# Four row tiles of attention probabilities: a fifth chunk of keys through the squares instead of TensorE's turns

## The reference

```python
def attention(x, ctx, wq, wk, wv, wo):      # per batch
    q, k_new, v_new = x @ wq.T, x @ wk.T, x @ wv.T
    k = concatenate([ctx, k_new])           # 512 + 512 keys
    v = concatenate([ctx, v_new])
    p = softmax(q @ k.T / sqrt(512))        # the mask is all false and not used
    return (p @ v) @ wo.T
x = x + tanh(g_xattn) * attention(layernorm(x), ...)
h = relu(layernorm(x) @ sign(up).T * up_scale)
x = x + tanh(g_ffn) * (h @ sign(down).T * down_scale) * output_scale
```

## Time and profile before

| | |
|---|---|
| median of three runs | 579.07 us |
| the profiled execution | 578.94 us |
| its span, from the first to the last instruction | 577.1 us |
| mean granted TensorE clock | 0.999 of full speed (2.4 GHz) |
| busy: TensorE, its weight loads | 571.5 us, 474.7 us |
| busy: VectorE, ScalarE, GpSimd | 397.4 us, 281.1 us, 125.7 us |
| DMA | 59.97 MB, 93248 packets, 71840 of them under 512 bytes |

### The profile page before, as it was taken

The page is one execution under the profiler, slowest core; times in us unless marked ns, Lnnn a source line. Parts: engine busy times, 40 slices in busy tenths (PEclk is TensorE's granted clock), DMA queues, the critical chain, the costliest instruction groups (busy, mean ns, idle before and its releaser), DMA issues.

```text
span 577.1 us, 6906 instructions
## 1 busy us (share of the span) xinstructions
PE 571.5 (99%) x2610; PEld 474.7 (82%) x2610; DVE 397.4 (69%) x556; ACT 281.1 (49%) x402; POOL 125.7 (22%) x111
## 2 busy tenths in 40 slices
PE   9999999999999999999999999999999999999997
PEld 7888888888888888888888888888888888888885
DVE  5889646688685588683588686777569645766654
ACT  3783513464321564321565454756468355555531
POOL 5006222102033002033002033332322022422002
PEclk9999999999999999999999999999999999999999
DMA  8711752124414145425113833273910311330011
GB/s 290 244 69 33 187 182 74 35 75 109 111 65 82 40 180 146 109 76 73 57 53 104 247 124 109 92 164 110 212 44 36 147 37 37 108 112 36 6 67 74
DMA packets 93248, 59.97 MB, mean 104 GB/s; under 512 B 71840, under 2 KB 75936, under 8 KB 92832
## 3 DMA queue, kind: packets, MB, share of 16 engines
q1 hardware_dynamic: 93216, 59.54, 35.4%
HBM read 44.84 MB, written 14.69 MB: 103 GB/s over the span
## 4 chain that ended last, share of the span: by engine, by line
PE 97%; DVE 1%; DMA 0%; ACT 0%; issue 0%
PE proj L680 28%; PE score L796 20%; PE turn L781 13%; PE score L714 9%; PE score L680 8%; PE turn L680 8%; PE proj L781 5%; PE proj L714 4%; PE score L922 2%; PE turn L672 1%; PE score L672 1%; DVE rows L1787 1%; DMA rows<-in_x 0%; DVE scaled L1784 0%; DVE stats L1615 0%; PE score L929 0%
## 5 line engine op out<-in xcount | busy, mean ns | idle before, releaser
L796 PE MATMUL score<-down_signs,hid_split 128*128 128x512 f32 x512 | 133.3, 389 | 0.0
L796 PEld LDWEIGHTS score<-down_signs,hid_split 128*128 128x128 f32 x512 | 96.0, 188 | 20.3 <-DVE hid_split L1668 0.5
L680 PE MATMUL proj<-four_x,weights 128*128 128x512 f32 x336 | 76.8, 389 | 0.0
L680 PEld LDWEIGHTS proj<-four_x,weights 128*128 128x128 f32 x336 | 63.0, 188 | 13.0
L604 POOL TENSOR_TENSOR four_x<-raw_ctx,four_x 128x2048 fp32r<-128x2048 f32 x7 | 32.6, 4656 | 132.0 <-ACT four_x L1010 132.0
L1668 DVE TENSOR_TENSOR hid_split<-hid,hid_split 128x512 fp32r<-128x512 f32 x64 | 44.4, 697 | 15.4 <-ACT hid_split L1226 15.1
L781 PE MATMUL turn<-ops_b,up_ops 128*128 128x512 f32 x192 | 51.3, 389 | 0.0
L1226 ACT ACTIVATE hid_split<-hid 128x512 fp32r<-128x512 f32 x64 | 40.0, 629 | 20.8 <-PE score L796 17.9
L1217 ACT ACTIVATE hid<-hid,hid_gain 128x512 f32<-128x512 f32 x48 | 34.7, 724 | 22.7 <-DVE hid L1697 11.1
L680 PE MATMUL score<-weights,four_x 128*128 128x512 f32 x192 | 45.3, 389 | 0.0
L680 PE MATMUL proj<-weights,four_x 128*128 128x512 f32 x192 | 45.3, 391 | 0.0
(11 more groups left out here) (140 smaller groups left out, 928.1 us busy)
## 6 DMA issues: line engine op xcount, KB each, us to landing
raw_w<-in_ffn_w SPq DMA_DIRECT2D x21, 512.0 KB, 3.3
raw_ctx<-in_ctx_turned SPq DMA_DIRECT2D x4, 1024.0 KB, 5.3
raw_ctx<-in_ctx SPq DMA_DIRECT2D x4, 1024.0 KB, 6.5
probs_rows<-probs_squares SPq DMA_DIRECT2D x64, 64.0 KB, 1.9
squares_placed<-probs_rows SPq DMA_DIRECT2D x8, 512.0 KB, 4.2
raw_x<-block_rows SPq DMA_DIRECT2D x4, 1024.0 KB, 7.3
result<-rows SPq DMA_DIRECT2D x16, 256.0 KB, 2.1
rows<-in_x SPq DMA_DIRECT2D x3, 1024.0 KB, 9.3
```

What stands on the lines that cost most here:

```text
L680: last = pe.matmul(bank, lhs(l), rhs(r), start=start and i == 0, stop=stop and i == 2)
L796: last = pe.matmul(wide(r), hid_split[:, n % HR, s, r * P:(r + 1) * P], down_signs[:, chunk_of(q), :], start=(q == 0 and s == HI), stop=(q ...
```

## The change

FAR gives each row tile the number of key chunks that go by the squares: five for all four, so the fifth is the first chunk of new keys. TensorE turns three chunks of a tile. `probs_squares` moves to another place of the memory, where the query parts lie, grows from 512 to 640 columns and for this its first write waits for another product of the scores. The loads of `squares_placed` have five chunks, and the second half is split by ScalarE and VectorE in two steps of one row tile each, so the counts of `placed_hi` and `placed_lo` become three per batch. The sync queue stores three tiles, loads the first half, stores the fourth tile and loads the second half. ScalarE's first split no longer waits for the stores. On TensorE the new product makes terms 1 to 3 of all four outputs first, then waits for the squares, and then makes the moved term 0 of all four, ahead of the context product.

```diff
--- before.py
+++ after.py
@@ -160,17 +160,23 @@
         late_squares = normed
 
 
+        FAR = dict.fromkeys(range(RT), RT + 1)
+        FAR_ALL = RT + 1
         PAIRS = ((2, 3), (0, 1))
-        probs_squares = at("probs_squares", 160, [P, RT, ROWS])
+        probs_squares = at("probs_squares", 112, [P, RT, FAR_ALL * P])
         squares_placed = at("squares_placed", 176, [P, KC, ROWS])
-        probs_rows = nc.dram_tensor("probs_rows", (BATCH, ROWS, ROWS), F32).ap()
+        probs_rows = nc.dram_tensor("probs_rows", (BATCH, FAR_ALL * P, ROWS), F32).ap()
         probs_rows_v = probs_rows.rearrange("b (c p) q -> b p c q", p=P)
         probs_squares_v = probs_rows.rearrange("b (j n) (t i a) -> b t i n j a", n=SQ, i=P // SQ, a=SQ)
 
         def placed_part(h):
 
             first = PAIRS[h][0] * P
-            return slice(None), slice(0, RT), slice(first, first + 2 * P)
+            return slice(None), slice(0, FAR[PAIRS[h][0]]), slice(first, first + 2 * P)
+
+        def split_part(k):
+
+            return placed_part(0) if k == 0 else (slice(None), slice(0, FAR_ALL), slice((k - 1) * P, k * P))
 
         def scaled(c, r):
 
@@ -230,6 +236,9 @@
                 return proj[:, n - 2, :] if n >= 2 else turn[:, n, :]
 
             return turn[:, n % 4, :] if n % 4 < 2 else score[1][:, n % 4 - 2, :]
+
+        def turned_cols(n):
+            return 4 * P if n < RT else KEYS - FAR[TILE_ORDER[n % RT]] * P
 
         def proj_bank(n):
             if n < DC:
@@ -450,18 +459,27 @@
 
             def place_squares(b):
 
-                for h, pair in enumerate(PAIRS):
-                    for t in pair:
-                        sp.wait_ge(probs_squared, tile_done(b, t))
-                        for i in range(P // SQ):
-                            sp.dma_start(probs_squares_v[b, t, i], probs_squares[i * SQ:(i + 1) * SQ, t].rearrange(
-                                "n (j a) -> n j a", a=SQ)).then_inc(squares_stored[h], 16)
+                def store_tile(t):
+                    sp.wait_ge(probs_squared, tile_done(b, t))
+                    far = FAR[t] * P // SQ
+                    for i in range(P // SQ):
+                        sp.dma_start(probs_squares_v[b, t, i][:, 0:far],
+                                     probs_squares[i * SQ:(i + 1) * SQ, t, 0:far * SQ].rearrange("n (j a) -> n j a", a=SQ)
+                                     ).then_inc(squares_stored[t not in PAIRS[0]], 16)
+
+                def place(h):
+                    sp.wait_ge(squares_stored[h], 2 * STORED * (b + 1))
+                    first, last = PAIRS[h]
+                    sp.dma_start(squares_placed[placed_part(h)],
+                                 probs_rows_v[b][:, 0:FAR[first], first * P:(last + 1) * P]).then_inc(placed[h], 16)
+
+                for t in TILE_ORDER[:3]:
+                    store_tile(t)
 
                 sp.wait_ge(scored, product_scored(b, A22, 1))
-                for h, pair in enumerate(PAIRS):
-                    sp.wait_ge(squares_stored[h], 2 * STORED * (b + 1))
-                    cols = slice(pair[0] * P, (pair[1] + 1) * P)
-                    sp.dma_start(squares_placed[placed_part(h)], probs_rows_v[b][:, :, cols]).then_inc(placed[h], 16)
+                place(0)
+                store_tile(TILE_ORDER[3])
+                place(1)
 
             def block_rows_back(b):
                 sp.wait_ge(squares_out[b], STORED)
@@ -673,7 +691,7 @@
                 last.then_inc(turned, 1)
 
             def cols(src):
-                return [src[:, k * P:(k + 1) * P] for k in range(4)]
+                return [src[:, k * P:(k + 1) * P] for k in range(src.shape[1] // P)]
 
             def product(bank, lhs, rhs, start, stop):
                 for i, (l, r) in enumerate(PASSES):
@@ -754,7 +772,7 @@
             def turn_probs(b, i):
                 t = TILE_ORDER[i]
                 pe.wait_ge(exp_done, tile_done(b, t))
-                turn_job(turn0(b) + i, cols(probs[:, t, ROWS:KEYS]))
+                turn_job(turn0(b) + i, cols(probs[:, t, FAR[t] * P:KEYS]))
 
             def v_jobs(b):
 
@@ -861,17 +879,20 @@
                 n = proj0(b)
                 pe.wait_ge(turn_lo, turn0(b) + RT)
 
+
                 for e in range(DC):
                     if e == 1:
                         pe.wait_ge(proj_lo, values_out(b, 3))
-                    for i, (lhs, rhs) in enumerate(new_terms(e)):
+                    for i, (lhs, rhs) in enumerate(new_terms(e)[1:]):
                         if e == 0:
 
-                            pe.wait_ge(proj_lo, values_out(b, max(i, 2)))
+                            pe.wait_ge(proj_lo, values_out(b, max(i + 1, 2)))
                         last = product(proj_bank(n + DC + e), lhs, rhs, i == 0, False)
+                pe.wait_ge(placed_lo, 3 * b + 3)
+                for e in range(DC):
+                    last = product(proj_bank(n + DC + e), *new_terms(e)[0], False, False)
                 if last_batch:
                     last.then_inc(new_read, 1)
-                pe.wait_ge(placed_lo, 2 * b + 2)
                 pe.wait_ge(ctx_ready, values_split(b) + 1)
                 for e in range(DC):
                     for i, (lhs, rhs) in enumerate(old_terms(e)):
@@ -1011,7 +1032,7 @@
 
             def turn_out(n, dst):
                 act.wait_ge(turned, n + 1)
-                act.activation(dst, four(turn_bank(n)), ACT.Copy).then_inc(turn_hi, 1)
+                act.activation(dst, four(turn_bank(n)[:, 0:turned_cols(n)]), ACT.Copy).then_inc(turn_hi, 1)
 
             def proj_out(n, dst):
                 act.wait_ge(proj_done, n + 1)
@@ -1093,15 +1114,13 @@
 
             def probs_out(b, i):
                 t = TILE_ORDER[i]
-                turn_out(turn0(b) + i, probsT[:, HI, RT:KC, t * P:(t + 1) * P])
+                turn_out(turn0(b) + i, probsT[:, HI, FAR[t]:KC, t * P:(t + 1) * P])
 
             def placed_out(b, h):
                 act.wait_ge(placed[h], 16 * (b + 1))
-                part = placed_part(h)
-                if h == 0:
-
-                    act.wait_ge(squares_stored[1], 2 * STORED * (b + 1))
-                act.activation(probsT[:, HI][part], squares_placed[part], ACT.Copy).then_inc(placed_hi, 1)
+                for k in ((0,), (1, 2))[h]:
+                    part = split_part(k)
+                    act.activation(probsT[:, HI][part], squares_placed[part], ACT.Copy).then_inc(placed_hi, 1)
 
             def take_signs(n):
                 kind, i = SIGNS[n]
@@ -1301,7 +1320,7 @@
 
             def turn_out(n, dst):
                 dve.wait_ge(turn_hi, n + 1)
-                dve.tensor_tensor(dst(LO), four(turn_bank(n)), dst(HI).bitcast(F32), ALU.subtract
+                dve.tensor_tensor(dst(LO), four(turn_bank(n)[:, 0:turned_cols(n)]), dst(HI).bitcast(F32), ALU.subtract
                                   ).then_inc(turn_lo, 1)
 
             def proj_out(b, i, dst):
@@ -1385,19 +1404,20 @@
 
             def probs_out(b, i):
                 t = TILE_ORDER[i]
-                turn_out(turn0(b) + i, lambda s: probsT[:, s, RT:KC, t * P:(t + 1) * P])
+                turn_out(turn0(b) + i, lambda s: probsT[:, s, FAR[t]:KC, t * P:(t + 1) * P])
 
             def square_probs(b, t):
                 dve.wait_ge(exp_done, tile_done(b, t))
                 if t == TILE_ORDER[0]:
-                    dve.wait_ge(scored, product_scored(b, S1, 1))
-                dve.transpose(probs_squares[:, t, :], probs[:, t, 0:ROWS]).then_inc(probs_squared, 1)
+                    dve.wait_ge(scored, product_scored(b, A22, 1))
+                dve.transpose(probs_squares[:, t, 0:FAR[t] * P], probs[:, t, 0:FAR[t] * P]).then_inc(probs_squared, 1)
 
             def placed_low(b, h):
-                dve.wait_ge(placed_hi, 2 * b + h + 1)
-                part = placed_part(h)
-                dve.tensor_tensor(probsT[:, LO][part], squares_placed[part], probsT[:, HI][part].bitcast(F32),
-                                  ALU.subtract).then_inc(placed_lo, 1)
+                for k in ((0,), (1, 2))[h]:
+                    dve.wait_ge(placed_hi, 3 * b + k + 1)
+                    part = split_part(k)
+                    dve.tensor_tensor(probsT[:, LO][part], squares_placed[part], probsT[:, HI][part].bitcast(F32),
+                                      ALU.subtract).then_inc(placed_lo, 1)
 
             def keys(b):
```

## The result

The changed kernel takes 591.19 us, the median of six runs (589.75 to 593.23), against 579.15 for the kernel before in six runs of its own (578.88 to 579.49). The ratio is 1.0211, with a 95% interval of 1.02 to 1.0221. I had forecast 583.8 in a range of 580.0 to 587.5, slower with a chance of 0.80. So the direction was right, and the size was outside the range: the kernel lost 12.0 us where I had summed 4.7.

What follows compares the result with a forecast made beforehand. TensorE was taken to bound the kernel, its gaps going one for one into the end. Turns, fourth-tile wait and value chunk 3 made +1.0, waits for the squares +3.7: 579.07 + 4.7 = 583.8 us, range 580.0 to 587.5.

Steps and rivals of the forecast that it cites:

- parts 1 to 3: TensorE's removed turns, fourth-tile wait and reordered new product: -0.44, +0.26 and +0.43 us per batch, +1.0 us in all.
- Removing the turns: On TensorE, sixteen transposes go at 0.109 us each: 0.44 us per batch, 1.75 us in all.
- the fourth tile's wait: VectorE's longer squares delay tile 1's maximum, so TensorE waits 0.26 us before the fourth tile's first transpose, bounds 0 to 0.35.
- value chunk 3: In the new product, wanted after 6 matmuls and no longer 9, so TensorE waits 0.43 us per batch, bounds 0.35 to 0.5.
- The order on the queue: On the sync queue, tile 1's stores land only after the first load of the squares, which delays the second load.
- the squares stay hidden: Rival, chance 0.18: tile 1's stores land 1.9 us after issue, second load follows after 4.2, only +1.0 remains, 580.1 us.
- the time that I had drawn from the Trainium skill: With pipelined descriptors, a later one need not wait for earlier writes; squares would stay hidden, 580.1 us.
- part 4: The squares' way through stores, loads and splitting: TensorE waits 0.7, 1.1, 0.5 and 1.4 us, 3.7 in all.
- My 6.0 us: On the sync queue, time from the first load's issue until tile 1's stores have landed and the second load can go.
- landing and splitting: Second load's landing, 3.9 us, then splitting by ScalarE and VectorE until the last low part, 2.2 us, 3.3 in batch 0.
- such hold-ups I leave as they are: On the sync queue, one store was held 2.08 us in its issue; the forecast kept such delays unchanged.
- issue time follows the pieces: Rival, chance 0.10: sync-queue stores take 0.68 us each to issue, 1.6 us more per batch, 590.2 us.

Runs made afterwards that it cites:

- four_chunks: The changed kernel with four chunks by the squares and four turns in every tile; new order, split and early wait kept: 581.02 us, ratio 1.0035.
- big_stores: The changed kernel with five-chunk squares and stores, but loads, copies and subtractions of four chunks, the fifth never read back: 584.88 us, ratio 1.0103.

## Where the prediction was right, and where it failed

**What bounds, and parts 1 to 3: right.** TensorE's gaps went one for one into the end, as the sum assumed. Removing the turns brings 1.5 us (1.75 predicted), the fourth tile's wait is 0.21 (0.26), value chunk 3's is 0.48 (0.43), and by itself it costs 1.3 us (1.7).

**The order on the queue: right.** The four stores issued behind the first load land late, in 4.4 us in batch 0, where stores ahead of it take 2.1. The rival "the squares stay hidden", with landings of 1.9 and a second load after 4 us, is refuted by that row, and so is the time that I had drawn from the Trainium skill (DMA: Bandwidth & Descriptors, Two DMAs through the same engine are not ordered). What the section says, that a later descriptor need not wait for an earlier one's writes, stands: in batch 1 the load issued at 149.57 and the store issued behind it at 150.10 land after

```profile
DMA to landing us min/median/max: 5.7/5.7/5.7
...
DMA to landing us min/median/max: 4.8/4.8/4.8
```

so the store is in at 154.9 and the load at 155.3. It passed the load by 0.4 us and was late all the same.

**The failed step: part 4's price of the quarter more data.** I wrote "Going up by a quarter I take 0.04 more each" for the stores, which is a price of their issue, and for the landing of the load ahead of tile 1's stores "I leave the extra quarter out here". My 6.0 us were 4.2 for that load to land and 1.8 for the four stores behind it. At the old sizes that is right: 4.3 and 1.6, 5.9 in all (four_chunks). At the new ones it is 5.1 and 2.2, 7.3 in all. What the sum left out is 128 KB more of load, and 64 more of stores in 128-byte pieces, ahead of the second load; enlarging the stores alone costs 0.7 of it, and the load alone 0.8. With 7.3 in place of 6.0 my own sum would have been 583.8 + 4 x 1.3 = 589, outside the range that I gave.

One thing in it stays open. One of the four stores is held in its issue in every batch, and whether that hold adds to the 7.3 or only shows it is not separated. In batches 2 and 3 the held store lands 0.5 and 0.4 us behind its neighbour, as the others do; in batch 0 it lands 1.5 us behind.

Term by term, against the working of part 4, in us per batch:

| | batch 0 | 1 | 2 | 3 |
|---|---|---|---|---|
| wait as predicted | 0.7 | 1.1 | 0.5 | 1.4 |
| second load behind the first, 6.0 predicted | +1.5 | +1.65 | +1.1 | +0.8 |
| first load earlier than predicted | -0.1 | -1.5 | -1.0 | -0.15 |
| first store nearer to TensorE's product | +0.2 | +0.2 | +0.2 | +0.2 |
| landing and splitting, 6.1 predicted (7.2) | +1.25 | +0.15 | +0.3 | +0.4 |
| sum | 3.5 | 1.6 | 1.1 | 2.6 |
| measured | 3.67 | 1.70 | 1.21 | 2.72 |

The first row of differences is the failed step. The second is luck, against "such hold-ups I leave as they are". Before, a store among the first twelve was held in its issue for 1.67 us in batch 1 and for 1.40 in batch 2. After the change those twelve go through in 6.9 and 6.8 us with none held, and the store that is held stands behind the first load. So the first load goes 1.5 and 1.0 us earlier than I had it, and the second does not. In the landing and splitting, batch 0 has an error of its own: I took 3.3 us from landing to the last low part, and it was 4.3, because the second subtraction ran beside GpSimd and took 1.89 us where its neighbour took 0.82. I had looked there for the tanh alone.

**What the sum did not have: the clock.** One fall behind batch 3's gap is 1.6 of the 10.9 us, and in half of the runs there are more. Predicted 4.7, plus 5.6 for the squares, plus 1.6 makes 11.9, 1.0 over what this span shows. Of that the turns' stretches gave back 0.6 more than I had, and a gap of the weight loads is not quite the gap of the matmuls (11.2 us of waits in the new products for 10.55 of growth).

**The rival "issue time follows the pieces"** named a time near the true one (590.2) for a wrong reason. It had 0.68 us a store. The twelve stores ahead of the load take 0.57 each in batch 0, against 0.54 in the kernel before, close to the 0.04 more that I took; it is one store behind the load that is held. And the range was too narrow for the same reason as the forecast: it had both loads at their longer price, but no term for stores standing behind a longer load, and none for the clock. The landing of the second load was not the error (3.9 taken, 4.1 measured). Stores that weigh 0.7 and a load 0.8, where four_chunks shows a cover of 0.0 to 1.2 us, come again in each of four batches.

**Cover that held.** The next rows of batch 0 and the blocks of batch 3 came later and TensorE did not wait for them, as I had said.

## What to carry to other kernels

When a transfer grows, price it at its new size in every place of the chain: in its issue, for whatever stands behind it on the DMA engines, in its landing, and in the instructions that read it; where the queue's order makes one depend on the next these add up. A wait that is moved forward spends cover that no busy share shows, and when it is spent, a further delay is paid. Load ahead of the stores only what somebody needs sooner, and count the full data of the load against those stores.

## What the runs showed of the hardware that I had not expected

- **A second queue did not bring small stores past a large load.** The stores on the sync queue landed in 4.3 us behind a load that ScalarE's queue had issued a microsecond earlier (batch 0; 4.5 to 5.1 in batches 1 and 2, with the load itself at 6.7 and 6.3), in 4.4 behind one of their own queue, and in 2.1 ahead of it.
- **A store can be held in its issue.** In the changed kernel one of the four stores behind the load took 1.93, 2.47, 2.10 and 2.25 us to issue, in batches 0 to 3. At the old sizes none of these four is held (2.3 to 2.4 us for all four in each batch), and with the load on the other queue one took 2.33. But a load ahead is not needed for it: the kernel before holds one store for 1.67 us in batch 1 and one for 1.40 in batch 2, where the sync queue had issued only other stores of the squares for four us and more (and one for 2.08 in batch 3). What it waits for no run settles.
- **VectorE slows down beside GpSimd.** A subtraction of 128x640 took 1.89 us for 0.82, and when the row gain stood in its place that took 1.05 for 0.23; in both GpSimd ran a subtraction of its own at the time. The Trainium skill (SBUF — State Buffer, Who interferes with whom) says that the two engines share a pair of ports which the one that starts first keeps for its whole instruction. The rows agree: VectorE's second subtraction starts at 73.8, while GpSimd's first (73.38, 1.59 us) runs until 74.97, and ends 0.7 us after that, about its own duration.
- **A gap of a few microseconds can cost more than itself.** Behind the 2.72 us of batch 3 the granted clock went to 1.2 GHz for some 3.4 us, which costs 1.7; behind 3.67 us in batch 0 of the same execution it stayed at 2.4 GHz. The length of the gap alone does not tell: in the profiled executions falls stand behind gaps of 2.44 to 3.89 us, and gaps of 2.87 (big_stores, batch 0) and 3.67 (the kernel after, batch 0) have none behind them. By the mean clocks it differs from run to run of the same kernel, and it is part of why a kernel that repeated within 0.6 us spread over 3.5.
